# Router logits as eight more columns of two products of a fused convolution, attention, state-space and expert kernel

## What is computed

```python
# attention over each image of 1024 tokens
q = (x * dw1) @ pw1 + b1;  v = (x * dw2) @ pw2 + b2
t = softmax(q @ q.T) @ v * gamma + x
# state-space mixer on the normed tokens
u = layernorm(t); xn = rmsnorm(u, norm_w)
z, xBC, dt = split(xn @ W_in.T); xBC = silu(causal_conv(xBC, 4 taps))
state = state * exp(dt * -exp(A_log)) + dt * x outer B; y = state @ C + D * x
y = rmsnorm(y * silu(z), gnorm_w)
t = t + u + y @ W_out.T
# experts: two of eight
f = layernorm(t)
p = softmax(f @ router_w.T); top 2, gates renormed
out = t + sum over the two of gate * (silu(f @ w1.T) * (f @ w3.T)) @ w2.T
```

## Time and profile before

| what | value |
|---|---|
| median of 3 runs | 1275.35 us |
| profiled execution, own time | 1275.21 us |
| its span, first to last instruction | 1273.4 us |
| busy: TensorE products | 1108.5 us (87%) |
| busy: VectorE | 866.5 us (68%) |
| busy: ScalarE | 702.8 us (55%) |
| busy: GpSimd | 601.8 us (47%) |
| mean granted TensorE clock | 0.942 of 2.4 GHz |
| instructions | 28242 |

### The profile page before, as it was taken

The page is one execution under the profiler, slowest core; times in us unless marked ns, Lnnn a source line. Parts: engine busy times, 40 slices in busy tenths (PEclk is TensorE's granted clock), DMA queues, the critical chain, the costliest instruction groups (busy, mean ns, idle before and its releaser), DMA issues.

```text
span 1273.4 us, 28242 instructions
## 1 busy us (share of the span) xinstructions
PE 1108.5 (87%) x7784; PEld 963.3 (76%) x7785; DVE 866.5 (68%) x2843; ACT 702.8 (55%) x1748; POOL 601.8 (47%) x860
## 2 busy tenths in 40 slices
PE   3899999999999999999999998872399999999950
PEld 2689889888888888888888888762288888888740
DVE  2578887888877887887888777754255555555534
ACT  1576776667767677676666666622144444444420
POOL 7123342564565466556457465555444444444320
PEclk8999999999999999999999999875699999999975
DMA  7100000001001001001000000001222222222249
GB/s 216 28 1 26 10 2 26 18 16 37 17 13 39 8 23 39 10 23 39 5 22 15 18 12 14 12 11 34 55 59 58 58 58 58 58 58 58 57 119 305
DMA packets 73174, 55.21 MB, mean 43 GB/s; under 512 B 9797, under 2 KB 67693, under 8 KB 73069
## 3 DMA queue, kind: packets, MB, share of 16 engines
q1 hardware_dynamic: 55437, 32.15, 9.6%
q0 software_dynamic: 8448, 17.45, 4.3%
q10 hardware_dynamic: 9184, 4.33, 1.2%
HBM read 31.21 MB, written 23.22 MB: 43 GB/s over the span
## 4 chain that ended last, share of the span: by engine, by line
PE 53%; DVE 14%; POOL 12%; issue 12%; ACT 5%; DMA 2%; SPq 1%; POOLq 0%; DVEq 0%; ACTq 0%
PE pX L520 6%; PE pY L522 6%; PE pc L371 5%; PE pa L427 4%; PE pb L537 4%; PE pd L537 4%; PE pc L529 4%; POOL rows_by_expert L896 3%; DVE CV L1020 2%; PE pY L333 2%; ACT PR L613 2%; POOL st L878 2%; DVE NM L1041 2%; PE pc L375 1%; PE pa L382 1%
## 5 line engine op out<-in xcount | busy, mean ns | idle before, releaser
L908 POOL DMA_INDIRECT results_by_choice<-YE,DIX x136 | 130.5, 960 | 190.7 <-ACT YE L719 178.4
L1261 DVE COPY V<-pc 128x384 f32<-128x384 f32 x136 | 75.8, 558 | 133.4 <-PE pc L529 132.1
L896 POOL DMA_INDIRECT rows_by_expert<-XA,SL x128 | 142.3, 1112 | 38.0 <-issue 28.1
L371 PEld LDWEIGHTS pc<-XDT,M 128*128 128x128 f32 x1024 | 130.1, 200 | 17.9 <-issue 13.4
L1020 DVE SCALAR_TENSOR_TENSOR CV<-XBC,cw,CV 128x256 f32<-128x256 f32 x288 | 140.5, 540 | 0.2 <-issue 0.2
L371 PE MATMUL pc<-XDT,M 128*128 128x64 f32 x1024 | 127.7, 280 | 10.7 <-DVE OFF L998 10.0
L427 PE MATMUL pa<-V,PT 128*128 128x128 f32 x1024 | 128.1, 278 | 3.6 <-DVE XDT L1077 3.5
L839 POOL TENSOR_TENSOR YG<-Y,SZ 128x256 f32<-128x256 f32 x64 | 46.5, 726 | 172.2 <-DVE Y L1062 170.0
L427 PEld LDWEIGHTS pa<-V,PT 128*128 128x128 f32 x1024 | 120.0, 192 | 9.6 <-issue 5.7
L520 PE MATMUL pX<-W,TA 128*128 x272 | 104.4, 465 | 0.9 <-ACT TA L706 0.7
L522 PE MATMUL pY<-W,TA 128*128 x272 | 101.1, 454 | 0.0
(11 more groups left out here) (250 smaller groups left out, 2902.9 us busy)
## 6 DMA issues: line engine op xcount, KB each, us to landing
GX<-rows_by_expert SPq DMA_DIRECT2D x136, 65.0 KB
XT<-in_xT_dram SPq DMA_DIRECT2D x8, 512.0 KB, 3.9
X<-in_x_dram SPq DMA_DIRECT2D x16, 256.0 KB, 3.0
W<-results_by_choice SPq DMA_DIRECT2D x8, 512.0 KB, 8.7
out_dram<-T ACTq DMA_DIRECT2D x8, 512.0 KB, 7.3
results_by_choice<-YE,DIX POOLq DMA_INDIRECT x136, 2.2
rows_by_expert<-XA,SL POOLq DMA_INDIRECT x128
W<-in_w1T_dram SPq DMA_DIRECT2D x1, 1364.0 KB
```

Of the source, the lines that this page charges most:

```text
L371: mm(pc[:, 64 * h:64 * h + 64], M[:, h, :], XDT[:, e % 2, HD * h:HD * h + 64], start=h == 0, stop=False, skip_group_check=True)
L896: g.indirect_dma_start(xg, bass.IndirectOffsetOnAxis(ap=SL[:, j // NT, j % NT:j % NT + 1], axis=0), XA[:, j // NT, j % NT, :], None).then_ ...
L908: g.indirect_dma_start(yg, bass.IndirectOffsetOnAxis(ap=DIX[:, j, :], axis=0), YE[:, j, :], None).then_inc(s(f"ye{j}_scattered"), 16)
```

## The change

The router logits are linear in the residual row before its second norm: t2 = TR + y @ wo with a factor RY per token, and TR is TA with a scale and a shift. So the kernel now takes router_w @ (normed row) from the z product (eight columns wz[:, 264:272] = routerT, scaled back by the new row 6 of `st`, to XR) and from the output product (eight columns wo[:, :, 128:136] = W_out.T @ routerT, made once at base 0, step 3), and adds them to LR. The mean is taken out with RB, the column sums of routerT, and the factor rs2 row 3.

```diff
-        wz, wx = sb("wz", [P, DI + H]), sb("wx", [P, 3 * P])
+        wz, wx = sb("wz", [P, DI + H + E]), sb("wx", [P, 3 * P])
...
-        wo = sb("wo", [P, 2, C])
+        wo = sb("wo", [P, 2, C + E])
...
-        st = sb("st", [P, 7, 4])
+        st = sb("st", [P, 2, 7, 4])
...
         @block.sync
...
+            load(wz[:, DI + H:], routerT)
...
         @block.tensor
...
-                    mm(pb[:, 0:DI + H], XNT[:, 0:P], wz[:], start=True, stop=True).then_inc(s("z_ps"), 1)
+                    mm(pb[:, 0:DI + H + E], XNT[:, 0:P], wz[:], start=True, stop=True).then_inc(s("z_ps"), 1)
...
-                if routes:
-                    upto(pe, "y2_ready", base, e + 1)
-                    rows_of_x(base, 0)
...
-                        last = mm(pb[:, 0:C], YT[:, m, :], wo[:, m, :], start=m == 0, stop=m == 1)
+                        last = mm(pb[:, 0:C + E], YT[:, m, :], wo[:, m, :], start=m == 0, stop=m == 1)
...
+                if base == 0 and i == 3:
+                    for m in range(2):
+                        last = nc.tensor.transpose(pd[:, P * m:P * m + P], wo[:, m, 0:C], ident[:])
+                    last.then_inc(s("woT_ps"), 1)
+                    pe.wait_ge(s("woT_ready"), 1)
+                    for m in range(2):
+                        mm(pd[:, 256 + E * m:256 + E * m + E], SQ[:, P * m:P * m + P], rT[:], start=True, stop=True, skip_group_check=True)
+                    mm(pd[:, 256 + 2 * E:256 + 3 * E], ones[:], rT[:], start=True, stop=True, skip_group_check=True).then_inc(s("woR_ps"), 1)
...
-                if routes:
-                    logits(base)
...
         @block.gpsimd
...
-            SPREAD = {(3, 3): (0, 1), (4, 1): (2,), (4, 2): (3,), (5, 1): (4,), (5, 2): (5,), (6, 1): (6,), (6, 2): (7,),
-                      (7, 1): (8,), (7, 2): (9,), (7, 3): (10,), (0, 1): (11,), (0, 2): (12,), (0, 3): (13,), (1, 1): (14,), (1, 2): (15,)}
+            SPREAD = {(3, 3): (0, 1), (4, 2): (2, 3), (5, 2): (4, 5, 6, 7), (7, 2): (8, 9, 10), (0, 2): (11, 12), (1, 2): (13, 14, 15)}
...
+                if i == 6 and there(base, -NT):
+                    norm_for_experts(base, 0, NT - 1)
...
+                    g.tensor_tensor(st[:, (fn // 2) % 2, 6, 2:4], st[:, (fn // 2) % 2, 0, 2:4], st[:, (fn // 2) % 2, 4, 2:4], ALU.mult)
...
                 if i == 6 and there(base, -NT):
-                    norm_for_experts(base)
+                    norm_for_experts(base, NT - 1, NT)
...
         @block.vector
...
+            def logits(base):
+                upto(dve, "rstd2_ready", base, 0)
+                tt(LG[:], LR[:], bc(rs2[:, 1, :]), ALU.mult)
+                routing[base - NT].did(tt(SA[:], bc(rs2[:, 3, :]), RB[:, None, :].broadcast_to([P, NT, E]), ALU.mult))
...
+                        ts(XR[:, (fb + j) % NT, :], bank[:, DI + H:DI + H + E], st[:, fpar, 6, j:j + 1], st[:, fpar, 6, 2 + j:3 + j], ALU.mult, ALU.mult)
...
+                    stt(LR[:, e % NT, :], pb[:, C:C + E], RY[:, 1, 0:1], XR[:, e % NT, :], ALU.mult, ALU.add)
                     t2 = T2[:, base + e, :]
                     stt(t2, pb[:, 0:C], RY[:, 1, 0:1], TR[:, e % NT, :], ALU.mult, ALU.add).then_inc(s("t2_ready"), 1)
+                if i in (4, 6) and there(base, NT):
+                    take_ql(base + NT, [i // 6])
                 if there(base, o):
                     upto(dve, "t_ready", base, o + 1)
                     v.bn_stats(BN[:, o % NT, :], TA[:, o % NT, :]).then_inc(s("bn_ready"), 1)
...
                     v.bn_aggr(MV[:, o % NT, :], BN[:, o % NT, :]).then_inc(s("mv_ready"), 1)
-                if i in (4, 6) and there(base, NT):
-                    take_ql(base + NT, [i // 6])
+                if base == 0 and i == 3:
+                    dve.wait_ge(s("woT_ps"), 1)
+                    v.tensor_copy(SQ[:], pd[:, 0:256]).then_inc(s("woT_ready"), 1)
+                    dve.wait_ge(s("woR_ps"), 1)
+                    v.tensor_copy(wo[:, :, C:], pd[:, 256:256 + 2 * E].rearrange("p (m e) -> p m e", m=2))
+                    v.tensor_copy(RB[:], pd[:, 256 + 2 * E:256 + 3 * E]).then_inc(s("woR_ready"), 1)
```

More of the change, by code:

```diff
@@ L946, in best, with shares, best_index @@
+            def shares(b):
+                routing[b].settle()
+                routing[b].did(tt(PB[:], PB[:], bc(r8[:, 2, :]), ALU.mult))
+            def best(b, js):
+                routing[b].settle()
                 apart(dve)
-                for j in range(NT):
+                for j in js:
                     last = v.max(M8[:, j, :], PB[:, j, :])
-                routing[base].then(last)
-            def best_index(base, js):
+                routing[b].did(last)
+            def best_index(b, js):
+                routing[b].settle()
@@ L955, in best_index, with one_hots @@
                     last = v.max_index(IX[:, j, :], M8[:, j, :], PB[:, j, :])
-                routing[base].did(last)
-            def one_hots(base):
-                steps = routing[base]
+                routing[b].did(last)
+            def one_hots(b):
+                steps = routing[b]
                 steps.settle()
@@ L1065, in step @@
                     last.then_inc(s("y2_ready"), 1)
-                if i == 1 and routes:
-                    best(base)
                 if front_b:
@@ L1085, in step @@
                     steps.did(v.reciprocal(dts[:, 9], dts[:, 4]))
+                if i == 0 and routes:
+                    sums(b)
                 if i == 2 and routes:
-                    both_best(base)
+                    both_best(b)
                 if front_b:
@@ L1100, in step @@
                     steps.did(ts(dts[:, 7], dts[:, 6], ATANH[4], None, ALU.mult))
+                if i == 0 and routes:
+                    best(b, range(4))
                 if i == 2 and routes:
-                    gates(base)
+                    gates(b)
                 if front_b:
@@ L1105, in step @@
                     steps.did(stt(dts[:, 8], dts[:, 7], ATANH[3], dts[:, 6], ALU.add, ALU.mult))
+                if i == 0 and routes:
+                    best(b, range(4, NT))
+                if front_b:
                     steps.settle()
@@ L1118, in step @@
                     tt(R1b[:], TOT, CUM, ALU.subtract).then_inc(s("dec_in"), 2)
-                if i == 1 and routes:
-                    best_index(base, range(3))
+                if i == 7 and there(base, -NT):
+                    logits(base)
                 if decays:
@@ L1128, in step @@
                     v.tensor_copy(C3[:, 1], R1[:]).then_inc(s("cum4"), 2)
+                if i == 7 and there(base, -NT):
+                    logits_max(base - NT)
                 if i == 1 and routes:
-                    best_index(base, range(6, NT))
+                    best_index(b, range(3, 6))
                 if decays:
@@ L1133, in step @@
                     tt(C3[:, 2], R1[:], C3[:, 1], ALU.subtract).then_inc(s("c3_ready"), 2)
+                if i == 7 and there(base, -NT):
+                    below(base - NT)
+                if i == 1 and routes:
+                    best_index(b, range(6, NT))
                 if there(base, k):
```

201 lines of the change are left out of this document (97 added, 104 removed).

## The result

The changed kernel takes 1295.78 us, the median of four runs (1293.07, 1294.11, 1297.46 and a disturbed one of 2271.88, which the ratio leaves out), against 1276.23 us for the kernel before: ratio 1.0147, 95% interval 1.0127 to 1.0167. It is slower by 1.5%, where the forecast was 1261 us, faster. The profiled execution took 1294.11 us with a span of 1292.3 us, so the sum is made against the span before, 1273.4: +18.9 us.

What follows compares the result with a forecast made beforehand. TensorE was taken as the bound. Terms -19.6, -3.9, -3.6, -2.8, +2.9, +10.5 and +2.8 summed to -13.7 us, from 1275.2 profiled (median 1275.35) to 1261 us; its own range 1250 to 1271, the stated range 1246 to 1272.

Steps and rivals of the forecast that it cites:

- Step 0, -19.6: Step 0 of seven batches loses transposes and narrow products on TensorE: 2.8 us each (bounds 1.4 and 3.2), -19.6 us in all.
- the low clock, -3.9: Three of four low-clock stretches of 1.3 us, each after the narrow products, were counted as gone: -3.9 us (bounds 0, -5.2).
- So 1.1 us of delay meets 0.3 us of slack: 0.75 in step 5: QL ahead of the statistics delays MV, st, XN and XDT: step 5 longer by 0.75 us (bounds 0, 1.1) in seven batches.
- Step 7, 0.75: Later st and factors (+0.5) and the softmax ahead of M (+0.4), partly overlapping: 0.75 us in each of seven batches.
- the clock falls elsewhere: Rival, chance 0.05: step 7's wait passes 2 us, low clock of 1.3 us in seven batches, none saved: 1274 us.
- over 2 us for YG: Sign that the forecast holds: TensorE waits over 2 us for GpSimd's YG in step 7, where it waited 1.78.
- Steps 1 to 3, -3.6: VectorE loses about 1.7 us of routing work in step 1: 0.6 us a batch (bounds 0, 1.1), six batches, -3.6 us.
- LR 0: VectorE's new eight-column operation per tile after the output product, costed at 0; with XR at most 21.8 us.
- The columns, +2.9: Eight more columns on three TensorE products of each tile, 15 ns each over 64 tiles: +2.9 us.
- The start, +2.8: Base 0, step 3: wo's transposes, copy and five products move L467 from 46.68 to near 49.5 us: +2.8 us.
- The end: After the last tile's statistics, scatter landings end slightly earlier and less work follows: last SL 2.8 us earlier.
- The rule weighed: VectorE and GpSimd share an exclusive port lock; rival, chance 0.03: GpSimd's 14 added instructions a batch block VectorE, 1281 us.

## Why the prediction was wrong

The sum was -13.7 us and the span grew by 18.9, 32.6 us apart. Undoing QL's place alone takes 26 us away, where the forecast had 10.5 for everything in steps 5 and 7.

**Step 0, -19.6 and the low clock, -3.9: right.** Six steps gave 23.3 us with their four low stretches, 3.1 each without them: the upper bound, not the 2.8 taken. All four low stretches went, not three; that six others came stands below.

**"So 1.1 us of delay meets 0.3 us of slack: 0.75 in step 5": this step failed.** MV came 1.05 us later, but that put st beside VectorE's CV products, which hold it for 1.15 us more. XN moved by 2.15, step 5 by 1.35, and step 4 itself by 0.4 (with QL behind MV it is 11.96, so LR has 0.14 of that and QL's place 0.26). The slack was read rightly: XDT moved by 1.88, 0.27 less than XN. I had priced a delay as a shift, with the length of every instruction taken from where it stood before. The hold was in the trace of before too, and I had not read it: in batch 5 the power of st took 1.05 us in step 4 and 2.18 in step 6, and the third st 0.19 in step 4 and 1.34 in step 2.

**Step 7, 0.75: the chain was right, and the clock behind it was left out of the sum.** The hold of step 6 was there before and after. MV was 1.13 us later and GpSimd had one instruction more in st; the block of the last tile's factors took 2.03 us where that of eight took 2.63, so 0.6 came back, not 0.3. YG stands 0.54 us later behind the NM of step 6, +0.5 in the forecast, the wait rose from 1.76 to 2.39, and behind it the clock fell: the rival "the clock falls elsewhere" came true in six batches beside everything else. The forecast itself had "over 2 us for YG" among its signs, which is the condition of that rival, and still gave it 0.05. In the run without XR and LR a step 7 with a wait of 2.36 us and the full clock took 13.72, no more than the 13.78 before the change, and with the low clock 14.92; VectorE's CV products were also not stretched in the first (below), and the two are not separated. Undoing QL's move takes the wait down to 1.1 us or away, with the softmax and the factors in two pieces still in place: 12.45 us where the power of step 6 is not held, 13.5 where it is, so these are no cost there.

**Steps 1 to 3, -3.6: the sign was wrong.** They cost 11.2 us in the six routed batches. I counted what left step 1 and not what came into step 0 ahead of MV (0.65 us), which ends in the hold and makes XN 1.1 us later, nor that the index search between the C3 operations makes VectorE longer from XDT to NM (8.54 to 9.27 us in batch 5). The wait for OFF grew from 6.7 to 7.7 us.

**XR 0: right. LR 0: low,** by 0.37 us in steps 0 to 6 of batch 5; the rest of the 4.0 us of the first stage is the clock's in the main. **The columns, +2.9:** in steps 0 and 1 of batch 1, which TensorE fills, nothing is seen (12.59 and 12.60, 11.24 and 11.24).

**The start, +2.8:** the product forecast near 49.5 us starts at 49.44, and step 3 of base 0 took 2.6 us more. Batch 0 as a whole took 6.9 more: undoing QL's move gave 2.7 of it back (step 5 7.79 and step 7 12.02 in place of 10.42 and 12.90), moving the set-up then 3.7, so the set-up cost more than its step. **The end:** from the last MV to the last SL it is 2.5 us shorter against 2.8 forecast; the other 2.8, of the step 0 at base 64, did not come: from the last NM to the last SL it is 2.1 in all. **Scatters, 0:** right only with this grouping. **The expert stage:** +4.6, not foreseeable from the change, cause open.

**The rule weighed.** I read the lock between the two engines only as GpSimd stopping VectorE, at 0.03. On the path of step 5 it was the other way round: a GpSimd instruction that meets three products of VectorE that read two SBUF tiles each (XBC and CV) ends only behind them. The Trainium skill (SBUF — State Buffer, Who interferes with whom) says that issue order decides who blocks, and that a VectorE instruction with two SBUF inputs contends with a GpSimd instruction that reads SBUF; the trace agrees with the second. Of the first it does not tell: the held instructions start 0.01 to 0.05 us ahead of the products in the rows, and are held all the same, so the starts in a trace do not show who had the ports first. In the other direction a power of 1.05 us, started 0.33 us ahead, left the three products at 1.26 us. GpSimd's bias of 512 columns did not, in step 7 of batch 5 before the change:

```profile
584.90 2.96 DVE L1020 SCALAR_TENSOR_TENSOR CV<-XBC,cw,CV 128x256 f32<-128x256 f32 x3
...
586.25 1.30 POOL L893 TENSOR_TENSOR X<-X,b2b 128x512 f32<-128x512 f32 x1
```

The changed kernel has the same there (2.99 us), so the change did not bring it.

## What to carry to other kernels

Price a moved instruction by what will stand beside it where it lands, above all for small GpSimd operations near runs of VectorE products from SBUF: starting 0.3 us earlier decided between 0.2 and 1.3 us here. Before moving work ahead of the statistics or factors of a chain over four engines, ask who waits behind them; the same 0.75 us of QL behind MV were free. Where a forecast wait reaches the condition of one of its own rivals, that rival belongs in the sum. And compare a step's length with its own parts (NM to XDT, XDT to NM), since each part has another owner.
